# Batch statistics from raw filter outputs, one joint scale and shift, and logits on every partition, in a memory-streaming kernel

## The reference

```
xl1 = _bn_relu(_dwconv(x, w1), g1, b1)      # x here is the group-normalised x
xl2 = _bn_relu(_dwconv(x, w2), g2, b2)
num = einsum('bck,bck->cb', xl1[:, :, 0, :], xl2[:, :, :, 0]).reshape(b, c)
num = (num @ lw1.T + lb1) @ lw2.T + lb2
num = softmax(num, axis=1)
out = x_in + x * num[:, :, None, None]
```

## Time and profile before

| what | value |
|---|---|
| three runs | 1706.28, 1706.61, 1708.42 us (median 1706.61) |
| the profiled execution | 1705.58 us, span of its instructions 1703.8 us |
| moved by DMA | 723.80 MB, mean 425 GB/s |
| busy, share of the span | DVE 59%, ACT 39%, POOL 30%, PE 28% |
| mean granted TensorE clock | 0.641 |

### The profile page before, as it was taken

The page is one execution under the profiler, slowest core; times in us unless marked ns, Lnnn a source line. Parts: engine busy times, 40 slices in busy tenths (PEclk is TensorE's granted clock), DMA queues, the critical chain, the costliest instruction groups (busy, mean ns, idle before and its releaser), DMA issues.

```text
span 1703.8 us, 14430 instructions
## 1 busy us (share of the span) xinstructions
PE 485.6 (28%) x3416; PEld 169.7 (10%) x3416; DVE 1004.7 (59%) x2672; ACT 665.1 (39%) x517; POOL 508.9 (30%) x489
## 2 busy tenths in 40 slices
PE   3588766660223321223333243430000000000000
PEld 1123212120001100001001021210000000000000
DVE  5899999967757576776666786772222222222220
ACT  4688887856435455544445546600000000000000
POOL 7678787820315444443254000000000000000000
PEclk8799878885666665666566566665555555555555
DMA  9999999989999999999999999999999999999999
GB/s 393 426 425 427 427 428 426 428 338 419 432 428 431 431 430 431 430 432 430 432 430 430 431 428 430 430 385 431 431 432 431 432 431 431 432 431 432 431 431 408
DMA packets 52126, 723.80 MB, mean 425 GB/s; under 512 B 6241, under 2 KB 6753, under 8 KB 8034
## 3 DMA queue, kind: packets, MB, share of 16 engines
q1 hardware_dynamic: 33922, 458.84, 63.4%
q10 hardware_dynamic: 18144, 264.25, 36.3%
HBM read 454.63 MB, written 268.44 MB: 424 GB/s over the span
## 4 chain that ended last, share of the span: by engine, by line
DMA 39%; another core or an unknown queue 26%; DVE 8%; PE 3%; issue 2%; ACT 2%; SPq 1%; DVEq 1%; POOL 0%; ACTq 0%; POOLq 0%
DMA xs<-in_x 28%; DMA out<-xs 11%; DVE xs L1104 3%; PE ps_part L576 2%; DVE xs L1028 1%; DVE mul_junk L1002 1%; DVE y2s L1031 1%; SPq L378 1%; ACT xs L878 1%; PE ps_part L710 1%; ACT sq_junk L805 1%; DVEq L1002 0%; DVE xs L1002 0%; POOL rstd_b L468 0%
## 5 line engine op out<-in xcount | busy, mean ns | idle before, releaser
L805 ACT ACTIVATE sq_junk<-xs 128x4096 fp8e5<-128x4096 f32 x128 | 463.1, 3618 | 203.9 <-DMA xs<-in_x 198.6
L576 PE MATMUL ps_part<-xs,filters 128*32 128x512 f32 x1856 | 290.8, 781 | 525.3 <-DMA xs<-in_x 516.2
L1104 DVE TENSOR_SCALAR xs<-xs,scale,shift 128x4096 f32<-128x4096 f32 x90 | 222.8, 2496 | 353.9 <-DMA xs<-in_x 353.3
L1002 DVE SCALAR_TENSOR_TENSOR xs<-xs,ps_w 128x256 f32 (+1 forms) x832 | 294.5, 416 | 28.6 <-DMA xs<-in_x 18.4
L534 POOL TENSOR_TENSOR xs<-xs,w_late 128x2048 f32<-128x2048 f32 x40 | 179.6, 4526 | 102.6 <-ACT w_late L819 102.6
L878 ACT ACTIVATE xs<-xs,shift,scale 128x4096 f32<-128x4096 f32 x33 | 125.3, 3798 | 157.3 <-DVE xs L1104 135.5
L576 PEld LDWEIGHTS ps_part<-xs,filters 128*32 128x32 f32 x1856 | 79.3, 138 | 718.3 <-issue 718.3
L1028 DVE TENSOR_TENSOR xs<-xs,ps_w 128x4096 f32<-128x4096 f32 x26 | 114.7, 4413 | 52.8 <-PE ps_part L576 46.6
L468 POOL TENSOR_TENSOR rstd_b<-var,minus_half 128x2 f32<-128x2 f32 (+1 forms) x23 | 15.2, 661 | 417.2 <-DVE var L1054 417.2
L1022 DVE TENSOR_REDUCE y2s<-xs 128x8 f32<-128x2048 f32 x40 | 91.4, 2286 | 77.1 <-POOL xs L534 77.1
L439 POOL TENSOR_TENSOR xs<-xs 128x768 f32<-128x768 f32 x64 | 116.7, 1827 | 58.0 <-DMA xs<-in_x 55.0
(11 more groups left out here) (116 smaller groups left out, 458.4 us busy)
## 6 DMA issues: line engine op xcount, KB each, us to landing
xs<-in_x SPq DMA_DIRECT2D x209, 2048.0 KB, 24.0
out<-xs ACTq DMA_DIRECT2D x121, 2048.0 KB, 27.6
filters<-in_x SPq DMA_DIRECT2D x5, 2048.0 KB, 18.0
out<-filters ACTq DMA_DIRECT2D x5, 2048.0 KB, 86.2
xs<-in_lw SPq DMA_DIRECT2D x2, 2048.0 KB, 16.3
out<-xs SPq DMA_DIRECT2D x2, 2048.0 KB, 12.1
filters<-in_w_rows SPq DMA_DIRECT2D x1, 512.0 KB, 3.8
filters<-in_w SPq DMA_DIRECT2D x1, 512.0 KB, 8.9
```

Source lines behind the costliest of these rows:

```text
L576: last = nc.tensor.matmul(ps_part[g % 2][32 * a:32 * a + 32, :], taps[:, g % 2, hf * JH + j, :], xs[:, s[0]:s[1] + 1:s[1] - s[0], j * W:(j ...
L805: nc.scalar.activation(sq_junk[:], xs[:, s, :], ACT.Square, accum_out=sq_sum[:, u % 2, u // 2, b:b + 1], saturate=False).then_inc(squared, 1)
L1002: return nc.vector.scalar_tensor_tensor(out=out, in0=x_row, scalar=1.0, in1=ps_w2[g % 2][:, 0:W], op0=ALU.mult, op1=ALU.mult, accum_out=total)
L1104: return nc.vector.tensor_scalar(buffer(s), buffer(s), scale[:, b, g:g + 1], shift[:, b, g:g + 1], ALU.mult, ALU.add)
```

## The change

- `normalise` goes. Batch statistics are taken on the raw filter outputs, four calls on 256 columns (a filter and a batch each) in place of two on 512, and DVE corrects them with small operations for the group's mean and deviation. POOL's `channel_factors` keeps one power. A new DVE helper `channel_affine` makes one joint scale and shift for each filter and batch, and DVE scales the column filter's output itself (two operations on 256 columns); ACT scales and rectifies the row filter's output alone. The rectifier of the other one goes into the dot product.
- The logits are summed on all 128 partitions: the weights of `add_logits` are a column spread to 128, the softmax runs on every partition, and each partition picks its own channel's logit by the mask `own`. `spread_prob` and its DVE steps go.
- Group 15 is filtered for each batch apart, with half the columns in a matmul.
- In `finish_row` the moments come ahead of the last fold, and the last quad's `turn_rows` is done in two parts: three groups ahead of the last unit's filter, one group after.
- Steps are called at other places: channel moments at 22 (before 24), the new affine step at 25 (24 in the second pass), `rectify` at 26 (24 in the second pass, before 27), dot products at 28 (27 in the second pass, before 28).

```diff
                 if q is not None:
...
+                    nc.gpsimd.tensor_tensor(own_rstd[:], var[:, width - B:width], minus_half[:, 0:B], ALU.pow
+                                            ).then_inc(own_ready, 1)
                     width -= B
                 factors(slice(0, width)).then_inc(rstd_ready, 1)
             def channel_factors(q):
...
+                pool.wait_ge(spread_ready, q + 1)
+                nc.gpsimd.tensor_tensor(bn_rstd[:], var_s[:], minus_half[:, 0:2], ALU.pow).then_inc(bn_ready, 1)
...
+                        pe.wait_ge(part_copied, 2 * g if g in (FG - 1, FG) else 2 * (g - 1))
+                if u == FIRST - 1:
+                    turn_rows(FQ - 1, range(QG - 1))
+                if g == FG - 1:
+                    for b in range(B):
+                        pe.wait_ge(x_loaded[s[b]], landed(s[b], ("x", u, b)))
+                        for j in range(JH):
+                            a = j % 4
+                            last = nc.tensor.matmul(
+                                ps_part[b][32 * a:32 * a + 32, 0:W], taps[:, g % 2, hf * JH + j, :],
+                                xs[:, s[b], j * W:(j + 1) * W],
+                                start=(hf == 0 and j < 4), stop=(hf == 1 and j >= JH - 4))
+                    last.then_inc(pe_read_x, 1)
+                    return
                 for b in range(B):
...
+            def turn_rows(q, groups):
+                end = QG * q + groups[-1] + 1
                 if q < FQ:
...
+                    pe.wait_ge(y2_done, 2 * end)
                 else:
...
+                    pe.wait_ge(rows_done, SETS * (4 * end + 1))
                 if q:
                     pe.wait_ge(dots_ready, 2 * q)
                 for e in range(E):
...
+                    for a in groups:
                         last = nc.tensor.matmul(
                             ps_y2[32 * a:32 * a + 32, :].rearrange("p (b e j) -> p b e j", b=B, e=E)[:, :, e],
                             sel[:, q % 2, e, :], y2s[:, (QG * q + a) % (2 * QG)], start=True, stop=True)
...
+                if groups[-1] == QG - 1:
+                    last.then_inc(y2_turned, 1)
             def moments(k):
                 q, width = quad_of(k), width_of(k)
...
+                        pe.wait_ge(logits_taken, row)
+                    nc.tensor.matmul(ps_l[:], one[:].to_broadcast([1, P]), bias[:], start=True, stop=False)
+                for b in range(B):
+                    pe.wait_ge(dots_ready, 2 * q + b + 1)
+                    last = nc.tensor.matmul(ps_l[:], dots[:, q, b:b + 1].to_broadcast([P, P]), mixed[:, B * h + b, :],
                                             start=False, stop=(q % FQ == FQ - 1 and b == B - 1))
                 if q % FQ == FQ - 1:
                     last.then_inc(logits_ready, 1)
...
             def finish_row(row):
                 q = FQ * (row + 1) - 1
+                moments(batch_of(QG * (q + 1) - 1, 1))
                 fold_parts(QG * (q + 1) - 1)
-                moments(batch_of(QG * (q + 1) - 1, 1))
-                turn_rows(q)
-                pe.wait_ge(bn_ready, q + 1)
-                keep_warm(3)
+                turn_rows(q, range(QG - 1, QG))
+                keep_warm(4)
                 add_logits(q)
-                keep_warm(2)
-                spread_prob(row)
...
             def rectify(q):
                 act.wait_ge(affine_ready, q + 1)
...
+                for b in range(B):
+                    half = slice(b * W, (b + 1) * W)
+                    nc.scalar.activation(z[:, half], ps_y1[:, half], ACT.Relu, scale=z_scale[:, 0, b:b + 1],
+                                         bias=z_shift[:, 0, b:b + 1]).then_inc(z_done, 1)
             def exponential(row):
                 act.wait_ge(exp_asked, row + 1)
...
+                nc.scalar.activation(z[:], ps_l[:], ACT.Exp, bias=neg_max[:], accum_out=exp_sum[:]).then_inc(exp_done, 1)
+                act.wait_ge(logits_taken, row + 1)
+                nc.scalar.activation(logit_g[:], logit_g[:], ACT.Exp, bias=neg_max[:]).then_inc(powers_done, 1)
             def scaled_by_act(s, g, done, count):
                 nc.scalar.activation(xs[:, s, :], xs[:, s, :], ACT.Identity,
...
+                if q is not None:
+                    nc.vector.tensor_tensor(own_off[:], nmean[:, width - B:width].unsqueeze(1).to_broadcast([P, 2, B]),
+                                            bc(tap_sum[:, q % 2, :, q // 2], B), ALU.mult)
             def channel_moments(q):
...
+                dve.wait_ge(folded, QG * (q + 1))
+                dve.wait_ge(y2_turned, q + 1)
+                for i, y in enumerate((ps_y1, ps_y2)):
+                    for b in range(B):
+                        last = nc.vector.bn_stats(bn_st[:, B * i + b], y[:, b * W:(b + 1) * W])
+                then_wait(last)
+                for i in range(2 * B):
+                    last = nc.vector.bn_aggr(bn_mv[:, i], bn_st[:, i])
+                then_wait(last)
+                dve.wait_ge(own_ready, q + 1)
+                mean, spread_of = (bn_mv[:, :, i].rearrange("p (i b) -> p i b", b=B) for i in range(2))
+                rstd = own_rstd[:].unsqueeze(1).to_broadcast([P, 2, B])
+                nc.vector.tensor_tensor(mean_b[:], mean, own_off[:], ALU.add)
+                nc.vector.tensor_tensor(var_b[:], spread_of, rstd, ALU.mult)
+                then_wait(nc.vector.tensor_tensor(off_b[:], own_off[:], rstd, ALU.mult))
+                nc.vector.tensor_tensor(mean_b[:], mean_b[:], rstd, ALU.mult)
+                then_wait(nc.vector.tensor_tensor(var_b[:], var_b[:], rstd, ALU.mult))
+                nc.vector.tensor_tensor(mean_d[:], mean_b[:, :, 0], mean_b[:, :, 1], ALU.subtract)
+                nc.vector.tensor_tensor(mean_s[:], mean_b[:, :, 0], mean_b[:, :, 1], ALU.add)
+                then_wait(nc.vector.tensor_tensor(var_s[:], var_b[:, :, 0], var_b[:, :, 1], ALU.add))
+                then_wait(nc.vector.scalar_tensor_tensor(out=mean_d[:], in0=mean_d[:], scalar=0.5, in1=mean_d[:],
+                                                         op0=ALU.mult, op1=ALU.mult))
+                nc.vector.scalar_tensor_tensor(out=gap_b[:], in0=bc(mean_s[:], B), scalar=-0.5, in1=off_b[:],
+                                               op0=ALU.mult, op1=ALU.add)
+                nc.vector.scalar_tensor_tensor(out=var_s[:], in0=mean_d[:], scalar=2 * EPS, in1=var_s[:],
+                                               op0=ALU.add, op1=ALU.add).then_inc(spread_ready, 1)
+            def channel_affine(q):
+                rstd = own_rstd[:].unsqueeze(1).to_broadcast([P, 2, B])
+                dve.wait_ge(bn_ready, q + 1)
+                then_wait(nc.vector.scalar_tensor_tensor(out=bn_a[:], in0=bn_rstd[:], scalar=2.0 ** 0.5,
+                                                         in1=affine[:, :, 0, q], op0=ALU.mult, op1=ALU.mult))
+                nc.vector.tensor_tensor(z_scale[:], bc(bn_a[:], B), rstd, ALU.mult)
                 for i in range(2):
...
+                    last = nc.vector.tensor_scalar(z_shift[:, i], gap_b[:, i], bn_a[:, i:i + 1], affine[:, i, 1, q:q + 1],
+                                                   ALU.mult, ALU.add)
+                last.then_inc(affine_ready, 1)
+                dve.wait_ge(affine_ready, q + 1)
+                for b in range(B):
+                    half = slice(b * W, (b + 1) * W)
+                    nc.vector.tensor_scalar(ps_y2[:, half], ps_y2[:, half], z_scale[:, 1, b:b + 1],
+                                            z_shift[:, 1, b:b + 1], ALU.mult, ALU.add).then_inc(y2_scaled, 1)
             def dot_products(q):
...
+                for b in range(B):
+                    half = slice(b * W, (b + 1) * W)
+                    dve.wait_ge(y2_scaled, 2 * q + b + 1)
+                    dve.wait_ge(z_done, 2 * q + b + 1)
                     nc.vector.scalar_tensor_tensor(
...
+                        out=z[:, half], in0=ps_y2[:, half], scalar=0.0, in1=z[:, half],
+                        op0=ALU.max, op1=ALU.mult, accum_out=dots[:, q, b:b + 1]).then_inc(dots_ready, 1)
             def softmax(row):
+                by_group = y_part[:, 0].rearrange("p (g c) -> p g c", c=CG)
                 dve.wait_ge(logits_ready, row + 1)
...
+                nc.vector.tensor_tensor(by_group, ps_l[:].rearrange("p (g c) -> p g c", c=CG),
+                                        own[:].unsqueeze(1).to_broadcast([P, G, CG]), ALU.mult)
+                nc.vector.reduce_max(neg_max[:], ps_l[:], AX.X, negate=True).then_inc(exp_asked, 1)
+                dve.wait_ge(exp_asked, row + 1)
+                nc.vector.tensor_reduce(logit_g[:], by_group, AX.X, ALU.add).then_inc(logits_taken, 1)
                 dve.wait_ge(exp_done, row + 1)
...
+                then_wait(nc.vector.reciprocal(exp_sum[:], exp_sum[:]))
+                dve.wait_ge(powers_done, row + 1)
+            def coefficients(row, half):
+                if half == 0:
```

(46 more changed lines are left out.)

158 lines of the change are left out of this document (40 added, 118 removed).

## The result

The changed kernel takes 1714.72 us (median of 6 runs, 1711.17 to 1717.22), the kernel before 1706.5 us beside it. The ratio is 1.0043, 95% interval 1.0033 to 1.0053: 7.3 us slower (5.6 to 9.1). Forecast were 1705.2 us and a range of 1701.0 to 1708.8. The profiled execution took 1716.83 us with a span of 1715.1.

What follows compares the result with a forecast made beforehand. The kernel was taken to be bound by memory traffic, with gains only in two pauses. 1705.58 - 2.4 (engine idle given back) + 1.0 (instruction packets) = 1704.2 profiled; with 1.03 to the median, 1705.2 us, range 1701.0 to 1708.8.

Steps and rivals of the forecast that it cites:

- (1): End of the first pass: group 15 filtered by batch, matmuls after the last landing 2.7 us instead of 5.4; -1.7 us.
- (2): End of first pass: moments ahead of the fold, starting 349.7 for 352.00, -2.3 us with (1); VectorE 1.1 us late.
- The recovery: First pass: VectorE work queued behind is made good at about 0.35 us a tile.
- (3): End of the first pass: statistics on raw outputs make the chain to the end of the logits 4.2 us shorter.
- (4): End of the first pass: softmax on all partitions takes 3.15 us instead of 4.20, -1.05 us.
- (5): Elsewhere: lighter ScalarE and GpSimd work, extra matmuls and moved steps stay hidden; ScalarE's queue 0 to 0.5 us late.
- What arrives: Of the 5.3 us shorter chain, up to 2.4 us arrives, since the sixteenth DMA engine works through the first pause.
- R1: Rival, chance 0.25: the first pause closes in full, 5.3 us less, 1701.3; with 3.3 of a second gap 1698.
- R2: Rival, chance 0.20: nothing arrives, as the sixteenth DMA engine is last at both pauses; median 1706.9 us.
- The term of -2.4 us: Second pause: idle time of the average DMA engine, given back if another engine is last there; up to 2.4 us.
- The added packets: Over both passes: two or three more instruction packets at 1.0 us, one on the last DMA engine; +1.0 us.
- R3: Rival, chance 0.13: slower, by instruction packets (1710) or, second, VectorE 9.3 us late at the first pass's end (+4.0).

Runs made afterwards that it cites:

- h1_last_only: The change applied only to the last quad of each pass, the six hidden quads left as in the kernel before; 1706.95 us, ratio 0.9996 to the kernel before.
- x1_psum: The changed kernel with one input of each small first-pass operation in PSUM, five operations more a quad; 1710.15 us, ratio 1.0009 to the kernel before.
- b3_early: The kernel before, with the first pass's kept tiles scaled by a constant right after the last dot product, softmax behind; 1705.85 us, ratio 0.9990.
- h2_tuned: h1_last_only with GpSimd's next filters built after VectorE's column scaling of row 0, and three more warming matmuls; 1706.93 us, ratio 0.9997 to the kernel before.
- b2_sbuf: The kernel before with 24 unused VectorE operations for each of the first three quads, both inputs in SBUF; 1733.29 us, ratio 1.0142.
- b2_psum: The kernel before with the same 24 unused operations a quad as b2_sbuf, but one input in PSUM; 1710.67 us, ratio 1.0011.
- b7_looped12: The kernel before with 12 unused VectorE operations behind each of the last pass's 64 scalings, in a loop; ratio 1.0025.
- b7_unrolled12: The kernel before with 12 unused VectorE operations behind each of the last pass's 64 scalings, written out; ratio 1.0017.

## Why the prediction was wrong

**The bound** was right: two pauses, both in the memory traffic.

**(1), (2), the start of the chain**, right where VectorE is on time. In h1_last_only the copy follows the landing by 3.6 us (before 5.5: -1.9, forecast -1.7), and the moments by 6.1 (before 8.8: -2.7, forecast -2.3 with lateness).

**(2), VectorE's lateness, is the step that failed.** "I take 1.1 us late at the end of the pass, within 0 and 3"; measured 12.5. The plain work was nearly right: moments 3.2 us for 1.6 and scale and shift 1.75 where nothing disturbs, 3.4 for the 3.1 forecast. What lacked is the wait for GpSimd, 11 us over three quads. I priced the small operations by the pair at 352.00 and 352.21. Both read PSUM, and GpSimd was idle then (its next instruction starts at 352.87). Neither holds for the new ones, with GpSimd busy 35.73 of 40 us. The recovery fell short too. Some 21 us were added and 12.5 were left, so 9 were made good over the 42 tiles from the first of these steps on, 0.2 us a tile for 0.35; x1_psum, without the waits, was still 4.3 us late.

**(3), (4), the chain** was to be 5.3 us shorter. It was 3.2 in the changed kernel, counted from the last row, and 0.7 and 3.5 in the two kernels with the last quad alone, counted from the last landing. "`keep_warm(4)` is free, since PE has nothing else between 350.9 and the dots, so I take 1.88" failed: 3.16 in the changed kernel and 3.78 in h1_last_only, for PE ran out of warming matmuls 3.2 and 3.9 us ahead. The lower clock had been priced, at 1.7.

**(5)** said the moved and lighter steps hide. GpSimd's relief was real but small (200.7 us busy for 204.4 between 100 and 343), but what it still did collided.

**What arrives**: right in kind. An earlier restart returned 1.7 of 7 us, or nothing clear of noise of 3.5, and the second pause took it back. R1 (chance 0.25), 5 to 6 us in the one and 3.5 in the other, is refuted; what h2_tuned shows is R2, nothing arrives. The term of -2.4 us was the right size at most: 1.7 in b3_early, 0.5 in h2_tuned, both uncertain by 1 to 2. (R1's 1701.3 was a time of the profiled execution and wasn't raised by 1.03 to the median, as the forecast was; that decided nothing.) The added packets were wrong: 33 before and after, where I had two or three more and 1.0 us. That fetching isn't hidden, which the prediction took from one packet beside one late landing, was not shown either.

**R3** is what happened, with a chance of 0.13, but by its second term alone: VectorE late beyond the stated break-even of 6.4 us. Its first, more packets of instructions, didn't occur. Its price, +4.0, came from 9.3 us of plain work, of which 3.4 us a quad were measured; the waits that made it 12.5 were not in it. The 12.5 less the 3.2 of a shorter chain are the 9.3 at the first scaling, but the profiled execution is 11.3 us longer: the late loads count, and the price took the chain alone. That a late start costs most of its delay while an early one returns little followed from my own reading of the pause, and I used it for the gain alone.

The sum of the parts by ratios: waits for GpSimd +0.34%, plain work and moved steps in the hidden quads +0.13% (x1_psum against h1_last_only), the new chains -0.04%: together +0.43%. The parts add up by construction; the last two are within or near their intervals.

## What to carry to other kernels

Before small operations are moved to VectorE, look at where their inputs lie and what GpSimd does meanwhile. Two inputs in SBUF beside a busy GpSimd cost up to 2.3 us each; with one input in PSUM they took 0.15 to 0.28. A duration for such an operation has to come from a row with the same memories and the same neighbour. And when fifteen of sixteen DMA engines pause, closing the pause was worth little here, while widening it cost up to the whole delay: price the two sides apart. A wait that a queue puts down to an engine isn't a loss while the DMA share stands at 1.0; look for the stretch where the share falls.

## What the runs showed of the hardware

A waiting small operation didn't get its turn at every end of a GpSimd instruction: the one of 2.29 us passed over four of them and ended with the fifth, ahead of a gap of 0.17 us. The same 128x4 operation took up to 1.81 us with both inputs in SBUF, and at most 0.16 with one in PSUM (b2_sbuf, b2_psum). A hardware loop on VectorE with a semaphore wait a turn took 0.38 us a turn (b7_looped12), the same operation written out 0.19 (b7_unrolled12). The first store moved 7 us earlier in b3_early, and the load 700 us later stood within 0.1 us of where it was.
